# A recurrent block on one Trainium2 core: weight preparation's products moved into the middle of in_proj's blocks, its last step behind the last taps, first loads in smaller pieces

## What is computed

```python
xn = _layernorm(x, axis=-1)
s = _L0_attn_ref(xn, ...)          # H 512, DIN 1024, N 16, R 32
g = _silu(_L0_ffn_ref(xn, ...))    # I 1376
x = x + s * g

# in the first branch
proj = hidden_states @ in_proj_w
x, z = jnp.split(proj, 2, axis=-1)
for k in range(K):                 # K = 4 taps
    xc = xc + conv_w[None, :, k:k + 1] * xp[:, :, k:k + Lq]
xc = jax.nn.silu(xc)
ssm_p = jnp.einsum('bdl,ed->ble', xc, x_proj_w)
# then rmsnorms, dt_proj, softplus, the scan over L, the gate silu(z), out_proj

# in the second branch, for gate, up and down
w = (q.astype(jnp.float32) - Q_ZERO) * (scale * Q_STEP)[:, None]
y = jnp.einsum('bsh,oh->bso', x, w)
return y + LR_SCALE * (x @ A @ Bm)
```

## Time and profile before

| | before |
|---|---|
| median of 3 runs | 1240.13 us |
| lowest, highest | 1240.11, 1247.17 us |
| the profiled execution | 1248.05 us |
| its span | 1246.2 us |
| PE busy | 1137.5 us (91%) |
| DVE busy | 1007.1 us (81%) |
| ACT busy | 698.4 us (56%) |
| POOL busy | 736.9 us (59%) |

### The profile page before, as it was taken

How to read it: one execution, slowest core, us unless ns; L and a number is a source line. 1 busy time by engine, 2 the same in 40 slices (tenths; PEclk the granted TensorE clock), 3 DMA queues, 4 the chain that set the end, 5 groups by cost and what they waited for, 6 DMA issues and landing times. The chain is left out here.

```text
span 1246.2 us, 12975 instructions
## 1 busy us (share of the span) xinstructions
PE 1137.5 (91%) x4430; PEld 602.0 (48%) x4430; DVE 1007.1 (81%) x832; ACT 698.4 (56%) x868; POOL 736.9 (59%) x408
## 2 busy tenths in 40 slices
PE   5887599999988999899999877999999899999998
PEld 3443255555544555555444333555555355555543
DVE  3786999999799999796404469999997999999630
ACT  3223767778765777672013385777878377777300
POOL 2000379999607999791220017999990589999311
PEclk9898899999999999899999988999999999999999
DMA  7553229999932899878711112899995359998851
GB/s 239 167 205 119 73 84 234 220 225 254 203 122 95 193 232 214 218 186 230 255 43 34 51 40 72 203 234 208 250 221 143 109 142 232 221 240 201 238 184 42
DMA packets 61059, 214.27 MB, mean 172 GB/s; under 512 B 6522, under 2 KB 6650, under 8 KB 60612
## 3 DMA queue, kind: packets, MB, share of 16 engines
q0 software_dynamic: 16128, 88.09, 36.0%
q1 hardware_dynamic: 43284, 119.70, 28.8%
q10 hardware_dynamic: 1584, 5.68, 1.1%
HBM read 102.52 MB, written 22.85 MB: 101 GB/s over the span
## 5 line engine op out<-in xcount | busy, mean ns | idle before, releaser
L581 POOL TENSOR_TENSOR ub<-dtx,bn 128x1024 f32<-128x1024 f32 x256 | 642.1, 2557 | 156.3 <-DMA bn<-ss_rows_scratch 70.2
L1214 DVE TENSOR_TENSOR_SCAN hb<-psA,ub 128x1024 f32<-128x1024 f32 x256 | 579.3, 2278 | 15.9 <-PE psT L971 7.7
L718 ACT ACTIVATE psA<-dt,cc 128x1024 f32<-128x1024 f32 x256 | 286.1, 1118 | 161.4 <-DVE hb L1214 120.5
L861 PE MATMUL psM<-xnT,w_ts 128*126 128x512 f32 x704 | 341.6, 615 | 37.0 <-DVE th L1077 30.5
L971 PEld LDWEIGHTS psT<-ident,hb 128*128 128x128 f32 x2048 | 234.1, 141 | 183.0 <-issue 86.4
L971 PE MATMUL psT<-ident,hb 128*128 128x128 f32 x2048 | 283.7, 277 | 18.3 <-DVE yT L1077 15.9
L739 ACT ACTIVATE yc<-psT,ssm 128x512 f32<-128x512 f32 x336 | 217.5, 677 | 56.1 <-PE psT L971 54.6
L861 PEld LDWEIGHTS psM<-xnT,w_ts 128*126 128x126 f32 x704 | 125.7, 196 | 154.0 <-issue 143.1
L993 PE MATMUL psM<-w_dn,hid 126*128 126x512 f32 x352 | 163.9, 594 | 0.0
L983 PE MATMUL psM<-xnT,w_ts 128*128 128x512 f32 x256 | 122.1, 602 | 6.2 <-DMA w_ts<-w_in_dram 6.2
L1077 DVE SCALAR_TENSOR_TENSOR yT<-psT,ssm,yT 128x512 f32<-128x512 f32 x144 | 104.9, 735 | 28.2 <-PE psT L971 26.6
(11 more groups left out here) (99 smaller groups left out, 704.9 us busy)
## 6 DMA issues: line engine op xcount, KB each, us to landing
yT<-yc POOLq DMA_DIRECT2D x112, 768.0 KB, 8.5
bn<-ss_rows_scratch SPq DMA_DIRECT2D x64, 512.0 KB, 6.3
w_ts<-w_gu_scratch SPq DMA_DIRECT2D x44, 504.0 KB, 4.4
w_ts<-w_in_dram SPq DMA_DIRECT2D x32, 256.0 KB, 7.1
hb<-z_scratch SPq DMA_DIRECT2D x16, 512.0 KB, 9.8
w_gu_scratch<-hid ACTq DMA_DIRECT2D x11, 504.0 KB, 4.2
yT<-x_dram SPq DMA_DIRECT2D x4, 1024.0 KB, 10.4
z_scratch<-th SPq DMA_DIRECT2D x16, 256.0 KB, 8.8
```

Source lines behind the costliest of these rows:

```text
L581: pool.tensor_tensor(ub[:, i % 2, :], dtx[:, i, :], bn[:, t, :], ALU.mult).then_inc(s_u, 1)
L718: act.activation(psA[:, i % 2, :], dt[:, i, :], ACT.Exp, scale=negA[:, h * DH + i, bass.ds(n, 1)]).then_inc(s_a, 1)
L861: mm = pe.matmul(psM[0:IM, gu, :], w_ts[:, t, at:at + IM], xnT[:, k, h * CH:(h + 1) * CH], start=(k == 0), stop=(k == HK - 1))
L1214: dve.tensor_tensor_scan(hb[:, t * DH + i, :], psA[:, i % 2, :], ub[:, i % 2, :], 0.0, ALU.mult, ALU.add).then_inc(s_scan, 1)
```

## The change

Six edits, nearly all in batch 0's beginning:

- `low_rank(j)` is issued in the block in which step j is used, the first step's product behind the first half of `x_part(m + 1)`, the second's behind the second half. The product is no longer a step ahead.
- Step 10 moves from block 6 to block 7, behind the last taps; its store on ScalarE's queue comes behind the copy of x_proj's result.
- Step 0 is dequantised before block 0's taps.
- First loads: `chan` first, then x in four pieces; the scales and the factors in two pieces each, first those of steps 0 to 3 (scales) or the first 512 columns (factors), the second ones later; `ln_w` last. The scale instruction is split to match.
- Statistics, roots and shifts are taken by quarters, in both batches, and `chan`'s exponential comes before them.
- The waits for all stores of gate and up move: SP loads the first two back before it, and VectorE waits for all before it writes `hid`. The wait for w_x moves to block 1.

The core of the diff:

```diff
-    return range(IT * m // (DB - 1), IT * (m + 1) // (DB - 1)) if m + 1 < DB else range(0)
+    first = [0, 1, 3, 4, 6, 7, 9, 10, IT]
+    return range(first[m], first[m + 1])
+QX = 4
+QB = TB // QX
+EARLY = 4 * 2 * IM
...
+            sp.dma_start(cc[:, :, :], chan).then_inc(s_const, 16)
             load_x(0)
-            sp.dma_start(cc[:, :, :], chan).then_inc(s_const, 16)
-            sp.dma_start(lnw[:, :], ln_w.to_broadcast([P, E])).then_inc(s_const, 16)
             load_w_in(0, 0)
-            sp.dma_start(scales[:, 0:2 * IT * IM], gu_s.to_broadcast([P, 2 * IT * IM])).then_inc(s_fc, 16)
-            sp.dma_start(scales[:, 2 * IT * IM:], dn_s.to_broadcast([P, H])).then_inc(s_fc, 16)
+            sp.dma_start(scales[:, 0:H], dn_s.to_broadcast([P, H])).then_inc(s_fac[0], 16)
+            sp.dma_start(scales[:, H:H + EARLY], gu_s[:, 0:EARLY].to_broadcast([P, EARLY])).then_inc(s_fac[0], 16)
             load_q(0)
             load_w_in(0, 1)
-            for it in range(1, QD):
-                load_q(it)
-            sp.dma_start(la, lr_a).then_inc(s_fc, 16)
-            sp.dma_start(lb, lr_b).then_inc(s_fc, 16)
+            load_q(1)
+            sp.dma_start(la[:, 0:H], lr_a[:, 0:H]).then_inc(s_lab[0], 16)
+            sp.dma_start(lb[:, 0:H], lr_b[:, 0:H]).then_inc(s_lab[0], 16)
+            load_q(2)
+            sp.dma_start(scales[:, H + EARLY:], gu_s[:, EARLY:].to_broadcast([P, 2 * IT * IM - EARLY])).then_inc(s_fac[1], 16)
             load_small()
+            sp.dma_start(lnw[:, :], ln_w.to_broadcast([P, E])).then_inc(s_lnw, 16)
...
+                        if m == 0:
+                            sp.dma_start(la[:, H:], lr_a[:, H:]).then_inc(s_lab[1], 16)
+                            sp.dma_start(lb[:, H:], lr_b[:, H:]).then_inc(s_lab[1], 16)
...
+                for t in range(2):
+                    if b == 0:
+                        sp.wait_ge(s_wst[t], 32)
+                    load_g(t, w_half(0, t), t)
                 if b == 0:
                     for t in range(QD):
-                        sp.wait_ge(s_wst[t], 16 + 16 * len(range(t, IT, QD)))
-                for t in range(2):
-                    load_g(t, w_half(0, t), t)
+                        sp.wait_ge(s_wst[t], stored(t))
...
+            act.wait_ge(s_const, 16)
+            act.activation(negA, negA, ACT.Exp).then_inc(s_negA, 1)
             layer_norm(0)
-            act.wait_ge(s_const, 32)
-            act.activation(negA, negA, ACT.Exp).then_inc(s_negA, 1)
...
                 act.activation(xr, psM[:, 0, :], ACT.Copy).then_inc(s_xr, 1)
+                if b == 0:
+                    for j in prepared(DB - 1):
+                        store_weights(j)
...
-                if b == 0:
-                    low_rank(0)
                 for m in range(DB):
-                    if m + 1 < DB:
-                        x_part(m + 1)
-                    if b == 0:
-
-                        for j in prepared(m):
-                            if j + 1 < IT:
-                                low_rank(j + 1)
+                    steps = list(prepared(m)) if b == 0 else []
+                    for c in range(HALVES):
+                        if m + 1 < DB:
+                            x_part(m + 1, c)
+                        if c < len(steps):
+                            low_rank(steps[c])
+                    if m == 1:
+                        pe.wait_ge(s_wx, 16 * b + 16)
                     if m > 0:
                         x_proj(m - 1)
...
+            dve.wait_ge(s_negA, 1)
+            dve.tensor_scalar(negA, negA, -1.0, None, ALU.mult).then_inc(s_prep, 1)
+            statistics(0, 0)
+            scale_shift(0, 0)
+            statistics(0, 1)
+            for q in range(2, QX):
+                statistics(0, q)
+                scale_shift(0, q - 1)
+            scale_shift(0, QX - 1)
+            step_scales(0, 0, H + EARLY, 2)
+            dequantise(0)
...
                         for j in prepared(m):
-                            dequantise(j)
+                            if j == EARLY // (2 * IM):
+                                step_scales(1, H + EARLY, H + 2 * IT * IM, 1)
+                            if j > 0:
+                                dequantise(j)
                             add_low_rank(j)
```

More of the change, by code:

```diff
@@ L625, in layer_norm @@
             def layer_norm(b):
-                for c in range(HALVES):
-                    half = slice(c * JD, (c + 1) * JD)
-                    act.wait_ge(s_mv, b * TB + (c + 1) * JD)
-                    act.activation(rs[:, half], mv[:, half, 1], ACT.Sqrt, bias=LN_EPS).then_inc(s_std, 1)
+                for q in range(QX):
+                    part = slice(q * QB, (q + 1) * QB)
+                    act.wait_ge(s_mv, b * TB + (q + 1) * QB)
+                    act.activation(rs[:, part], mv[:, part, 1], ACT.Sqrt, bias=LN_EPS).then_inc(s_std, 1)
                 for tb in range(TB):
@@ L1110, in dequantise @@
                 dve.wait_ge(s_q[turn % QD], 16 * (turn // QD) + 16)
-                stt(w_dn[0:IM, j, :], qs[turn % QD][0:IM, 0:H], -Q_ZERO, scales[0:IM, 2 * IT * IM:], ALU.add,
+                stt(w_dn[0:IM, j, :], qs[turn % QD][0:IM, 0:H], -Q_ZERO, scales[0:IM, 0:H], ALU.add,
                     ALU.mult).then_inc(s_deq, 1)
@@ L1124, in _, with step_scales @@
             psT_row = psT[:, :, :].rearrange("p a c -> p (a c)")
-            for c in range(HALVES):
-                statistics(0, c)
-                scale_shift(0, c)
+            def step_scales(part, lo, hi, loads):
+                dve.wait_ge(s_fac[part], 16 * loads)
+                dve.tensor_scalar(scales[:, lo:hi], scales[:, lo:hi], Q_STEP, None, ALU.mult).then_inc(s_scl, 1)
+                dve.wait_ge(s_scl, part + 1)
             dve.wait_ge(s_negA, 1)
             dve.tensor_scalar(negA, negA, -1.0, None, ALU.mult).then_inc(s_prep, 1)
-            dve.wait_ge(s_fc, 64)
-            dve.tensor_scalar(scales, scales, Q_STEP, None, ALU.mult).then_inc(s_scl, 1)
-            dve.wait_ge(s_scl, 1)
+            statistics(0, 0)
[7 more added lines that the diff above has]
+            dequantise(0)
             for b in range(NB):
@@ L1272, in _ @@
                         dve.wait_ge(s_out, b * (TB * 16) + 16)
+                        if b == 0:
+                            for t in range(QD):
+                                dve.wait_ge(s_wst[t], stored(t))
                         hidden(0, 0)
```

78 lines of the change are left out of this document (44 added, 34 removed).

## The result

| | before | after |
|---|---|---|
| median of the comparison (7 runs each) | 1245.85 us | 1229.29 us |
| lowest, highest | 1237.73, 1248.58 us | 1224.49, 1234.55 us |
| the profiled execution | 1248.05 us | 1229.79 us |
| its span | 1246.2 us | 1228.0 us |
| first reduction after in_proj of batch 0 | 118.47 us | 104.41 us |

A forecast was written before the change was run, and what follows sets the result against it. Bound by a dependent recurrence per batch, so savings in the first 118 us carry through. 2.2 + 5.2 - 1.1 + 4.15 = 10.45 at full clock, 15.1 with low-clock time; 11.1 expected from 1240.13: 1229.0 us, range 1223.5 to 1236.

The forecast's parts named there:

- rival (c): Batch 0's start: TensorE transposes two tiles early, waits some 3 us, stays at low clock; 1258 us; chance 0.03.
- The square: Sign at the end of batch 0's changed stage: if the prediction was right, this operation comes before 103 us.
- Start, 2.2 forecast: Batch 0's first loads to block 1's taps: TensorE no longer stops between blocks 0 and 1; taps 34.7 for 36.92.
- rival (b): First loads: chan needs 7.5 us at the head, statistics begin 3.9 late; gain 6.5, 1233.6 us; chance 0.08.
- Middle, 5.2 forecast: Blocks 2 and 4, one step each: low-rank products between in_proj's halves shorten the loop from 10.65 to 8.07, 2.58 twice.
- Rival (d): Blocks' in_proj: the middle placement does nothing because TensorE is full anyway; 1235 us; chance 0.08.
- Scale step, -1.1 forecast: VectorE ahead of step 4, in a two-step block: the scales' second part is uncovered, 1.06 us, a loss of 1.1.
- Last step, 4.15 forecast: Step 10 moved behind block 7's taps: block 6 then has one step and takes 8.25 us for 12.40.
- The bank wait, 0.0 to 0.8 forecast: After the last taps: x_proj's transposes wait for a PSUM bank the last addition reads; 0.0 as profiled, 0.8 at full clock.
- The half-clock time: TensorE's low-clock stretches in blocks 2 and 6 go with its long waits: 4.66 us of the profiled execution.
- case (a): Batch 0's blocks: the earlier runs had both low-clock stretches like the profiled one; gain 15.1, 1225.0 us; chance 0.25.
- Batch 1: Batch 1's statistics by quarters: 0.7 us more on VectorE, covered by 5.61 us of idle; cost zero.

## Why the prediction was right, and where its steps were not

The forecast was 1229.0 and the median is 1229.29. The mechanism was right; the agreement to 0.3 us is partly luck. The gain was put at 11.1 and is 14.1 at the mark, and the base of 1240.13 is 4.6 below the median of 31 runs; the two errors cancel for the most part.

**Marks of the profile.** Taps were forecast at 26.5, 34.7, 45.9, 54.0, 66.3, 74.3, 85.5, 93.8 and came at 27.07 to 94.97, each 0.4 to 0.9 late, the last 1.2. The clock was full up to 97 and beyond. TensorE did transpose two tiles early and then waited 2.29 us for the copies (to 12.94), as rival (c) has it, but the granted clock stayed at 1.00. It waited 0.78 and 0.69 for `w_dn`, the first copy was at 12.22 for 12.5. The square was at 103.78, after the 103 given. The profiled execution, put at 1233, took 1229.79; the kernel it is compared with had 4.1 us more behind the mark.

**Start, 2.2 forecast.** x was usable at 5.48 for 5.7, and `chan` had landed by 3.14, so rival (b) with its 7.5 at the head did not occur. Nor did the four pieces of x pay for themselves one after the other: VectorE began on them at 5.48, 7.53, 8.95 and 10.57. In_proj began at 18.41 for 18.1. Block 1's taps came 1.8 us earlier (35.09 for 36.92), for 2.2. What I did not see is that block 0 becomes longer with it: without step 0 dequantised beforehand VectorE does that work under TensorE's product and in_proj (7.53 for 8.02). With the second scale step's price 0.8 of it is left at the mark, 1.1 by my two terms.

**Middle, 5.2 forecast.** The loop of 8.07 measured 8.24 and 8.25 (blocks 2 and 4), so the two gains at full clock are 10.65 less these, 2.4 each, 4.8. The placement also did what I had booked elsewhere: it took the low level away (4.66, most of it left out of the forecast) and block 6's wait of 1.19. Together 10.7; measured from the first taps on with step 10 still in block 6 it is 90.95 - 80.06 = 10.9 (the new start alone, and the changed kernel with step 10 back). Rival (d), that it does nothing, is refuted by the kernel with the placement taken back.

**Scale step, -1.1 forecast.** By the prediction's own rule it is 1764/3284 of 1.87 = 1.00 us, not the 1.06 written there. It lasts 1.07 and lengthens block 3 by 1.12; 0.36 of that comes back in block 4, so it costs 0.8.

**Last step, 4.15 forecast.** The move by itself brought 2.35 at the mark and 2.7 from the first taps on, so this term was mis-sized. I subtracted the new block 6 from 11.21 + 1.19, but the 1.19, the wait for the product of step 10, goes with the placement and has nothing to do with the step's move; 11.21 - 8.61 = 2.6 is what the move is worth in the block. That moves 1.19 from one term to another and leaves the sum as it is; only the remaining 0.36, a block 6 of 8.61 for 8.25, is missing from the whole. With the products one step ahead block 6 lasts 12.25 with the move and 14.06 without, 1.8, and the marks of these two (117.11 and 116.84) show none of it, since the one with the move began 1.3 later and had 0.9 more in block 2. The bank wait, 0.0 to 0.8 forecast, was 0.5 to 0.65 at an x_proj of 1.30.

**The half-clock time.** Here the step failed. I argued from three runs, two of which agreed to 0.02 us, that executions near 1240 us lack the low-level stretches, and kept only 0.65 of the 4.66. Four executions with TensorE's old order were profiled (before twice, the placement taken back, the start alone); all have two or three such stretches before 100 us, also the one at 1240.33 us. None of the seven with the middle placement and the early dequantising has one before the wait in front of its last x_proj. So case (a)'s 15.1 was the right sum, and 14.1 of it came. The missing 1.0 is 0.3 in start and scale step (0.8 for 1.1), 0.4 in the two loops (4.8 for 5.2) and 0.36 in block 6. The low median of three was a draw: over 31 runs it is 1244.74, and 1244.74 - 14.1 = 1230.6. Against the record's 1240.13 the same gain would have given 1226.

**Batch 1.** Statistics by quarters were put at nothing; the taps of its first blocks were not tested by themselves, and the scatter there is larger than 0.7.

## What to carry to other kernels

When two engines hand work to each other inside a loop, try putting the product between two halves of a long piece that does not depend on it. The wait for the other engine then lies under the first half, and no engine has to run a step ahead. Here that was worth 12.6 of 14.1 us, by the estimate above nearly half of it through the clock. Count such a gain after the other edits, not beside them: the last step's move was worth 2.6 us, and not 4.15, once the placement had taken a wait out of its block. And if a kernel's total scatters by more than an edit is worth, read a mark behind the changed stage, which repeated here within 0.3 us where the time behind it differed by up to 14 between variants.

## What the runs showed of the hardware

- TensorE's waits of 2.36 to 2.72 us between its products were followed by the lower level of 1.2 GHz in 12 of 14 cases: 2.72 was (block 2 of the placement alone), 2.58 in the same place was not, 2.37 was at 71.22 in before's second execution, and 2.36 was not at 73.13 in its first. Waits of 0.7 to 0.9 never were. Against the 10.65 or 12.40 us of such a block at the full clock (8.26 for the placement alone), a drop cost 1.6 to 1.7 us in ten of the twelve, 2.5 in block 2 with the placement taken back (13.18 for 10.65) and 3.01 in before's block 2. What decides between these cases no run shows.
- GpSimd's four normalising tiles of 128x512 take 3.02 us alone and 4.72 beside VectorE's scaling and dequantising. These slow down too (the scaling 0.95 to 1.00, the dequantising 1.28 to 1.69).
- A wait for loads of w_in in the recurrence stage varies from nothing to 6.2 us between executions of one kernel, and the part behind the mark from 1119.3 to 1133.7 us between variants that do not touch it.
